# A fused attention and mixture-of-experts layer: head pairs as straight-line units, coarse scores in row tiles, routing moved among the attention units

## The chip, the core and the metric

The kernel runs on one core of one Trainium2 chip. Its time is device microseconds of that core, from launch to end, and lower is better. The core has five engines that run side by side and meet only at semaphores: TensorE (PE, matmuls into PSUM), VectorE (DVE), ScalarE (ACT), GpSimd (POOL) and SyncE (SP), which here issues all DMAs. PSUM has eight banks of 512 fp32 columns.

## The reference

Eight sequences of 512 tokens, width 128, pass one post-norm layer. Sixteen heads of width 64; eight experts of width 256, two of them chosen for each token.

```python
q, k, v = (einsum('bsd,hdk->bhsk', x, w) for w in (w_q, w_k, w_v))
weights = softmax(einsum('bhqk,bhmk->bhqm', q, k) / sqrt(64))
z = einsum('bhqm,bhmk->bhqk', weights, v)          # then heads side by side, times w_o
x1 = layernorm(x + (x + z @ w_o))
top_logits, top_idx = top_k(x1 @ gate_w, 2);  combine = one_hot(top_idx) * softmax(top_logits)
h = silu(einsum('bsd,edf->ebsf', x1, w1));  y = einsum('ebsf,efd->ebsd', h, w2)
out = layernorm(x1 + (x1 + einsum('ebsd,bse->bsd', y, combine)))
```

## The kernel before, in words

All data is fp32. Most matmul operands are split in a high part, rounded to the type fp32r, and a low part, the remainder; a `product` is three fp32r matmuls (high x high, high x low, low x high). `times_v` and `sum_probs` are plain fp32 matmuls, which the trace shows as two records each.

**Attention** goes over 64 head pairs n (8 sequences x 8 pairs). For a pair, q and k are projected as one 128-row tile (two heads of 64 rows) into the one bank `MISC`; ScalarE evicts the high part, VectorE the low one. SyncE then stacks high and low parts of each head by DMA into `q_stack` and `k_stack`, 128 rows for a head. *Coarse scores* (`coarse`, L519) are 8 matmuls a pair (2 heads x 4 tiles of 128 queries), from the stacks, into banks 4 and 5 in turn. VectorE reduces each to a row maximum (`maxima`, L1025), TensorE transposes the maxima (`shift_rows`, L537), VectorE copies them to a row (L1033), and a small DMA puts it into row 64 of the stack (`load_shift`, L284), so that the true scores (`scores`, L555 and L556) come out shifted. ScalarE takes exponentials of two banks at a time (`exps`, L858). GpSimd adds the four key tiles of each head (`add_probs`, L396). TensorE multiplies by v in four steps c that stand apart between other work (`times_v`, L567: two heads side by side, 64 output partitions each) and sums the probabilities over keys with a matrix of ones (`sum_probs`, L581), once a pair. ScalarE evicts the sums to `zT`, VectorE takes reciprocals in four pieces (L1040), and multiplies (`z_part`, L1045); ScalarE and VectorE split z (L871, L1050), TensorE projects out (`project_out`, L478 to L480) and VectorE adds into `acc` (L1061). All sequences are transposed at the start; `acc` holds all eight.

The order of work on each engine is written out by hand in `body(n, j)`. The first 8 and the last 2 pairs are straight-line, the rest a hardware loop over two pairs. Weights of a pair and x of a sequence are copied by DMA to fixed tiles (`load_wqk`, `load_wo`, `load_xT`), since a loop's addresses on TensorE are fixed.

**Experts** follow when attention has ended: steps k = 8b + e over sequences b and experts e (`chunk`). `hidden` (L478 to L480, 6 matmuls) runs three steps ahead, ScalarE applies silu into SBUF (L954), TensorE spreads the token weights c over partitions (`spread_c`, L725), VectorE gates (L1223), ScalarE and GpSimd split the result (`g_hi_part` L961, `g_lo_part` L426), and `second` (L735, L739) accumulates y over 8 experts. Among the steps stand, for later sequences: load of `acc`, transposes to tokens (L679), first norm (L1127, L1131, L1141, and GpSimd's power L422), transposes back, logits, routing (`route1` and `route2`, L1153 to L1185), transposed weights (`transpose_c`, L706); and for the former one the sum, second norm (L1232 to L1244) and store (L350).

## Time and profile before

| | |
|---|---|
| runs | median 1280.31 us of 3 (1279.3 to 1281.87) |
| profiled execution, span | 1280.0 us |
| busy: PE, DVE, ACT, POOL | 1196.7, 987.7, 602.0, 679.6 us |
| mean granted TensorE clock | 0.978 of full |
| moved by DMA | 153.47 MB |

The profile is of one execution. Busy time of an engine is the time in which an instruction of it ran; matmuls overlap, so a busy TensorE can still do more. "Idle before" is the time that the engine stood before an instruction, and the arrow names what ended it. A start-to-start distance in the timeline is what an instruction costs in a stream; its duration is longer, since it includes the way through the array. PE's granted clock has two levels, 1.2 and 2.4 GHz.

### The profile page before, as it was taken

Reading aid. Unit: us, or ns where it says so; the run is one execution under the profiler, and the core shown is the slowest. Engines: PE = TensorE matmul, PEld = TensorE weight load, DVE = VectorE, ACT = ScalarE, POOL = GpSimd, SP = SyncE. Lnnn points to the kernel's source line nnn. Section 1 sums busy time; section 2 is a strip of 40 time slices with the busy share of each in tenths; the row PEclk is TensorE's granted clock in tenths of the full one; section 3 lists DMA queues with packets and bytes.
Section 4 is the critical chain, followed back from the end, with each engine's and each line's share of the span. In section 5 each row is a group of like instructions: output and inputs, shape, how many; then the busy total and the mean of one; then the engine's idle time right before and its main releaser. Section 6 shows DMA issues by size and latency. Waiting matters only on the chain. (4 is left out here: it accounts for less than half of the span.)

```text
span 1280.0 us, 20247 instructions
## 1 busy us (share of the span) xinstructions
PE 1196.7 (93%) x4952; PEld 693.9 (54%) x4952; DVE 987.7 (77%) x1618; ACT 602.0 (47%) x744; POOL 679.6 (53%) x502
## 2 busy tenths in 40 slices
PE   5799999999999999999999999999998788888886
PEld 3454555555555555555555555555553566666664
DVE  4586888788888788888788888788887667777764
ACT  4444444444444444444444444444443555556553
POOL 0464644455544455544555544555546366666665
PEclk9898999999999999999999999999999889999999
DMA  9666666566665565665666665656660000000000
GB/s 213 162 161 153 157 155 157 144 156 147 157 156 140 144 155 146 158 159 153 150 150 153 159 148 140 150 149 152 160 161 21 21 9 17 17 17 16 8 9 17
DMA packets 91643, 153.47 MB, mean 120 GB/s; under 512 B 18016, under 2 KB 36960, under 8 KB 91616
## 3 DMA queue, kind: packets, MB, share of 16 engines
q1 hardware_dynamic: 91616, 153.14, 48.1%
q8 instruction: 13, 0.21, 0.1%
q14 instruction: 14, 0.11, 0.0%
HBM read 6.30 MB, written 2.10 MB: 7 GB/s over the span
## 5 line engine op out<-in xcount | busy, mean ns | idle before, releaser
L1025 DVE TENSOR_REDUCE neg_max<-psum 128x1 fp32r<-128x512 f32 x512 | 345.1, 680 | 114.1 <-PE psum L530 112.1
L1040 DVE RECIPROCAL zT<-zT 128x128 f32<-128x128 f32 x256 | 241.4, 944 | 4.2 <-ACT zT L865 2.2
L530 PE MATMUL psum<-k_stack,q_stack 128*128 128x512 f32 x512 | 224.6, 451 | 6.8 <-DVE neg_max L1025 1.4
L555 PE MATMUL psum<-q_stack,k_stack 128*128 128x512 f32 x512 | 210.5, 411 | 9.9 <-DMA q_stack<-q_stack 7.4
L858 ACT ACTIVATE probs_even<-psum 128x1024 f32<-128x1024 f32 x128 | 131.0, 1023 | 179.1 <-PE psum L556 179.1
L556 PE MATMUL psum<-q_stack,k_stack 65*128 65x512 f32 x512 | 205.2, 401 | 0.0
L396 POOL TENSOR_TENSOR probs_sum<-probs_even 128x512 f32<-128x512 f32 x64 | 82.5, 1289 | 227.4 <-PE psum L581 187.2
L396 POOL TENSOR_TENSOR probs_sum<-x_tok 128x512 f32<-128x512 f32 x64 | 82.2, 1284 | 226.9 <-PE psum L581 226.9
L530 PEld LDWEIGHTS psum<-k_stack,q_stack 128*128 128x128 f32 x512 | 97.1, 190 | 185.0 <-DVE neg_max L1025 87.9
L396 POOL TENSOR_TENSOR probs_sum<-probs_sum,probs_even 128x512 f32<-128x512 f32 x128 | 164.1, 1282 | 14.5 <-ACT probs_even L858 3.3
L396 POOL TENSOR_TENSOR probs_sum<-probs_sum,x_tok 128x512 f32<-128x512 f32 x128 | 164.3, 1283 | 11.3
L858 ACT ACTIVATE x_tok<-psum 128x1024 f32<-128x1024 f32 x128 | 130.9, 1023 | 41.7 <-PE psum L556 41.7
L567 PE MATMUL psum<-x_tok,v 128*64 128x512 f32 x512 | 139.7, 626 | 0.0
L567 PE MATMUL psum<-probs_even,v 128*64 128x512 f32 x512 | 137.9, 617 | 0.0
L1223 DVE TENSOR_TENSOR x_tok<-x_tok,psum 128x1024 f32<-128x1024 f32 x64 | 77.9, 1217 | 77.1 <-PE psum L725 48.1
L555 PEld LDWEIGHTS psum<-q_stack,k_stack 128*128 128x128 f32 x512 | 98.1, 192 | 45.8 <-issue 20.4
L865 ACT ACTIVATE zT<-psum 128x512 f32<-128x512 f32 x64 | 38.3, 598 | 171.0 <-PE psum L581 171.0
L556 PEld LDWEIGHTS psum<-q_stack,k_stack 65*128 65x128 f32 x512 | 98.0, 191 | 20.4
L426 POOL TENSOR_TENSOR k_stack<-x_tok,k_stack 128x1024 fp32r<-128x1024 f32 x32 | 76.9, 2404 | 54.6 <-ACT k_stack L961 54.6
L426 POOL TENSOR_TENSOR q_stack<-x_tok,q_stack 128x1024 fp32r<-128x1024 f32 x32 | 75.5, 2377 | 35.8 <-ACT q_stack L961 35.8
L847 ACT ACTIVATE v<-psum 128x1024 f32<-128x1024 f32 x32 | 32.9, 1027 | 128.5 <-PE psum L567 126.6
L954 ACT ACTIVATE x_tok<-psum 128x1024 f32<-128x1024 f32 x64 | 65.6, 1026 | 56.4 <-PE psum L480 55.4
(119 smaller groups left out, 1927.1 us busy)
## 6 DMA issues: line engine op xcount, KB each, us to landing
q_stack<-q_pair SPq DMA_DIRECT2D x128, 256.0 KB, 3.0
k_stack<-k_pair SPq DMA_DIRECT2D x128, 256.0 KB, 3.6
q_stack<-q_pair SPq DMA_DIRECT2D x128, 128.0 KB, 3.5
k_stack<-k_pair SPq DMA_DIRECT2D x128, 128.0 KB, 3.4
xT_cur<-xT SPq DMA_DIRECT2D x32, 512.0 KB, 3.0
wqk_cur<-w_tab SPq DMA_DIRECT2D x63, 256.0 KB, 3.3
wo_cur<-w_tab SPq DMA_DIRECT2D x64, 128.0 KB, 3.0
x_tok<-L_attn_x_dram SPq DMA_DIRECT2D x8, 256.0 KB, 5.4
```

Of the source, the lines that this page charges most:

```text
L396: nc.gpsimd.tensor_tensor(probs_sum[h][:], left, probs[j][:, h, c, :], ALU.add).then_inc(s["added"], 1)
L426: nc.gpsimd.tensor_tensor(g_lo[e % GB], gated[e % 2], bits(g_hi[e % GB]), ALU.subtract).then_inc(s["g_lo_done"], 1)
L530: nc.tensor.matmul(psum[:, COARSE + t % 2, :], q_stack[j][:, h, 0, t * P:(t + 1) * P], k_stack[j][:, h, 0, :], start=True, stop=True).then ...
L555: nc.tensor.matmul(psum[:, t, :], k_stack[j][:, h, 0, keys], q_stack[j][:, h, 0, :], start=True, stop=False)
L556: mm = nc.tensor.matmul(psum[:, t, :], k_stack[j][0:EXT, h, 1, keys], q_stack[j][0:EXT, h, 1, :], start=False, stop=True)
L567: mm = nc.tensor.matmul(psum[h * DK:(h + 1) * DK, Z, :], v[:, j, c, h, :], probs[j][:, h, c, :], start=(c == 0), stop=(c == TT - 1))
L858: nc.scalar.activation(probs[j][:, h, 2 * g:2 * g + 2, :], psum[:, 2 * g:2 * g + 2, :], ACT.Exp).then_inc(s["exp_done"], 1)
L865: nc.scalar.activation(zT[:], psum[:, MISC, :], ACT.Copy).then_inc(s["sums_out"], 1)
L954: nc.scalar.activation(silu[e % 2], psum[:, FC * (e % 2):FC * (e % 2 + 1), :], ACT.Silu).then_inc(s["silu_done"], 1)
L1025: nc.vector.tensor_reduce(neg_max[h][:, t:t + 1], psum[:, COARSE + t % 2, :], AX.X, ALU.max, negate=True).then_inc(s["max_done"], 1)
L1040: nc.vector.reciprocal(zT[:, cols], zT[:, cols]).then_inc(s["r_done"], 1)
L1223: nc.vector.tensor_tensor(gated[e % 2], silu[e % 2], psum[:, CB, :].unsqueeze(1).broadcast_to([P, FC, S]), ALU.mult).then_inc(s["gated"], 1)
```

## The change

The program is written anew. No hardware loops are left: every engine runs through units n = -2 .. 64 as straight-line code, then through 64 expert steps. The parts:

- `coarse` reads `q_pair` and `k_pair` (high parts only, 64 rows a head) instead of the stacks. The two heads' matmuls use rows 0 to 63 and 64 to 127 and write two banks; one `maxima` reduces both. One transpose and one row copy serve both heads.
- `times_v` of the former pair stands in one block, `sum_probs` once for two pairs, with 32 columns of ones, four tiles into one bank. ScalarE evicts 128 rows of sums, VectorE takes reciprocals (4 pieces for two pairs), and SyncE spreads them with 4 DMAs a pair (`spread_recip`). z is evicted by ScalarE (`z_part`), and GpSimd multiplies (`z_mul`) and makes the low part (`z_lo`).
- The copies of weights and x to fixed tiles are gone. x of later sequences is loaded and transposed among units; `acc` holds two sequences, and the first addition takes 2x in.
- First norm and routing of sequences 0 to 6 stand in attention units 8b + 11 to 8b + 15 (`norm_of`), those of the last one in the expert steps (`LAST_NORM`). The token weights go to DRAM and come back spread over 128 partitions (`spread_c`, by DMA). Logits are made with tokens on partitions.
- In the expert steps, silu is written in place in PSUM and the gate reads it there; y has two banks in turn.
- Experts' weights are loaded and split in four quarters in units 0 to 7.

The core of the diff, cut:

```diff
 # TensorE
-                nc.tensor.matmul(psum[:, COARSE + t % 2, :], q_stack[j][:, h, 0, t * P:(t + 1) * P], k_stack[j][:, h, 0, :],
-                                 start=True, stop=True).then_inc(s["coarse_done"], 1)
+            def coarse(m, t):
+                if t == 0:
+                    pe.wait_ge(s["qhi"], m + 1)
+                    pe.wait_ge(s["khi"], m + 1)
+                    n = m - 1
+                    if n > 0:
+                        pe.wait_ge(s["exp_done"], group(n - 1, 1, 1) + 1 if (n - 1) % 2 == 0 else group(n - 1, 0, 1) + 1)
...
+                for h in range(2):
+                    half = slice(h * DK, (h + 1) * DK)
+                    mm = nc.tensor.matmul(psum[:, coarse_pair(t) + h, :], q_pair[half, 0, t * P:(t + 1) * P], k_pair[half, 0, :],
+                                          start=True, stop=True)
+                mm.then_inc(s["coarse_done"], 1)
...
+            def times_v(n):
+                j = n % 2
+                pe.wait_ge(s["exp_done"], group(n, 1, 1) + 1)
+                pe.wait_ge(s["v_out"], n // 2 + 1)
+                wait(pe, s["acc_done"], n - 2)
+                pe.wait_ge(s["row_done"], min(n + 2, N))
+                for c in range(TT):
+                    for h in range(2):
+                        mm = nc.tensor.matmul(psum[h * DK:(h + 1) * DK, Z, :], v[:, j, c, h, :], probs[j][:, h, c, :],
+                                              start=(c == 0), stop=(c == TT - 1))
+                mm.then_inc(s["pv_done"], 1)
+            def sum_probs(k):
+                pe.wait_ge(s["added"], 6 * (2 * k + 2))
...
+                for i in range(4):
+                    mm = nc.tensor.matmul(psum[32 * i:32 * i + 32, M, :], ones[:], probs_sum[i // 2][:, i % 2, :], start=True, stop=True)
+            def project_out(m):
+                pe.wait_ge(s["zhi"], m + 1)
+                pe.wait_ge(s["zlo"], m + 1)
+                pe.wait_ge(s["row_done"], min(m + 5, N))
...
+            for n in UNITS:          # order of a unit (waits and bounds of n left out)
+                transpose_x(b), or to_tokens / transpose_x1 / logits / transpose_c of norm_of(n, step)
+                coarse(n + 1, 0); coarse(n + 1, 1)
+                times_v(n - 1)
+                if n % 2 == 0: sum_probs((n - 2) // 2)
+                coarse(n + 1, 2); coarse(n + 1, 3)
+                scores(n, 0, 0); project_q(n + 2); scores(n, 0, 1); project_k(n + 2); scores(n, 1, 0)
+                transpose_max(n + 1); project_out(n - 3); scores(n, 1, 1)
+                if n % 2 == 0: project_v(n)
 # ScalarE: order of a unit
+                z_part(n - 1); [even: sums_part((n - 2) // 2)]; zT_part(n - 3)
+                exps(n, 0, 0); q_part(n + 2); exps(n, 0, 1); k_part(n + 2)
+                exps(n, 1, 0); exps(n, 1, 1); [even: v_part(n)]
+            def zT_part(m):
+                act.wait_ge(s["zmul"], m + 1)
+                wait(act, s["wo_done"], m)
+                nc.scalar.activation(zT_hi[:], z_raw[:, m % 3, :], ACT.Copy).then_inc(s["zhi"], 1)
 # VectorE
-                    nc.vector.tensor_reduce(neg_max[h][:, t:t + 1], psum[:, COARSE + t % 2, :], AX.X, ALU.max,
-                                            negate=True).then_inc(s["max_done"], 1)
+                nc.vector.tensor_reduce(neg_max[:].rearrange("p (h t) -> p h t", h=2)[:, :, t], psum[:, bank:bank + 2, :], AX.X,
+                                        ALU.max, negate=True).then_inc(s["max_done"], 1)
+                maxima(n + 1, 0); maxima(n + 1, 1); [norm or routing part]; maxima(n + 1, 2); maxima(n + 1, 3)
+                q_part(n + 2); [even: reciprocal 0]; k_part(n + 2); row_part(n + 1); [even: reciprocal 1]
+                acc_part(n - 3); [even: reciprocals 2 and 3]
 # GpSimd: order of a unit
+                add_probs(n - 1, 1); [rstd_part(b)]; z_mul(n - 3); z_lo(n - 3); add_probs(n, 0)
+            def z_mul(m):
+                pool.wait_ge(recip_in[m % 2], 4 * DMA * (m // 2 + 1))
+                pool.wait_ge(s["z_out"], m + 1)
+                z = z_raw[:, m % 3, :]
+                nc.gpsimd.tensor_tensor(z, z, recip[:, m % 2, :], ALU.mult).then_inc(s["zmul"], 1)
 # SyncE
+            def spread_recip(m):
+                sp.wait_ge(s["recip_done"], TT * (m // 2 + 1))
+                wait(sp, s["zmul"], m - 1)
+                for h in range(2):
+                    i = 2 * (m % 2) + h
+                    for r in range(2):
+                        sp.dma_start(recip[h * DK + r * 32:h * DK + (r + 1) * 32, m % 2, :],
+                                     sums[32 * i:32 * i + 32, :]).then_inc(recip_in[m % 2], DMA)
+                [odd n: spread_recip(n - 3); spread_recip(n - 2)]; [expert quarter]
+                stack(0, n + 2, 0); shift(n + 1); stack(1, n + 2, 0); stack(0, n + 2, 1); stack(1, n + 2, 1)
 # expert steps
-                nc.scalar.activation(silu[e % 2], psum[:, FC * (e % 2):FC * (e % 2 + 1), :],
-                                     ACT.Silu).then_inc(s["silu_done"], 1)
+                nc.scalar.activation(h, h, ACT.Silu).then_inc(s["silu_done"], 1)      # h: the two PSUM banks
-                nc.tensor.matmul(psum[:, CB, :], select_e[:, e, :], cT[:, j, :], start=True,
-                                 stop=True).then_inc(s["cb_done"], 1)
+                sp.dma_start(c_b[:, e, :], c_dram[b, e:e + 1, :].broadcast_to([P, S])).then_inc(c_in[e], DMA)
+                nc.vector.tensor_tensor(gated[k % 2], psum[:, FC * (k % 2):FC * (k % 2 + 1), :],
+                                        c_b[:, e, :].unsqueeze(1).broadcast_to([P, FC, S]), ALU.mult).then_inc(s["gated_done"], 1)
```

The orders of a unit above are given as calls in a line; in the program each stands under its own condition on n. After the last unit the engines run the 64 expert steps: TensorE `hidden(k + 3)` and `second(k)`, ScalarE `silu_part(k + 2)` and `g_hi_part(k + 1)`, VectorE `gate_part(k + 2)`, GpSimd `g_lo_part(k)`, with the last two pairs' `z_mul`, `z_lo` and `project_out` among the first of them.

## Rows read from the trace of the kernel before

**Rows 1.** The page, parts 1 and 2: busy time and slices.
```profile
PE 1196.7 (93%) x4952; PEld 693.9 (54%) x4952; DVE 987.7 (77%) x1618; ACT 602.0 (47%) x744; POOL 679.6 (53%) x502
...
PEclk9898999999999999999999999999999889999999
```

**Rows 2.** Busy time in two stretches of the expert phase: PE, PEld, DVE, ACT, POOL, clock.
```profile
1100.00:1250.00 150.00, 131.68 (x563) 100.95 (x561) 106.71 (x202) 89.44 (x97) 94.23 (x52) 0.95 0.04 14
...
1097.00:1101.00 4.00, 3.81 (x12) 3.00 (x13) 3.13 (x11) 0.84 (x2) 1.29 (x3) 0.57 0.00 0
```

**Rows 3.** Timeline of TensorE, two head pairs in mid attention: start, duration, instruction.
```profile
501.87 0.28 PE L537 MATMUL psum<-ident,neg_max 128*4 128x128 f32 x1
...
502.69 0.40 PE L480 MATMUL psum<-xT,wqk_cur 128*128 x1
502.93 0.39 PE L530 MATMUL psum<-k_stack,q_stack 128*128 128x512 f32 x1
503.25 1.08 PE L567 MATMUL psum<-probs_even,v 128*64 128x512 f32 x4
...
526.68 0.28 PE L479 MATMUL psum<-w_tab,xT_cur 128*128 x1
526.80 0.28 PE L480 MATMUL psum<-w_tab,xT_cur 128*128 x1
...
531.33 0.28 PE L537 MATMUL psum<-ident,neg_max 128*4 128x128 f32 x1
```

**Rows 4.** Timeline of TensorE, last pairs: two steps of times_v together.
```profile
972.09 1.94 PE L567 MATMUL psum<-probs_even,v 128*64 128x512 f32 x8
...
973.86 1.03 PE L581 MATMUL psum<-probs_sum,ones 128*64 128x512 f32 x4
```

**Rows 5.** Groups by line and shape: busy us, mean ns, idle before and releasers.
```profile
L1025 DVE TENSOR_REDUCE neg_max<-psum 128x1 fp32r<-128x512 f32 x512 | 345.1, 680 | 114.1 <-PE psum L530 112.1
L1040 DVE RECIPROCAL zT<-zT 128x128 f32<-128x128 f32 x256 | 241.4, 944 | 4.2 <-ACT zT L865 2.2
...
L396 POOL TENSOR_TENSOR probs_sum<-probs_sum,x_tok 128x512 f32<-128x512 f32 x128 | 164.3, 1283 | 11.3
...
L858 ACT ACTIVATE probs_even<-psum 128x1024 f32<-128x1024 f32 x128 | 131.0, 1023 | 179.1 <-PE psum L556 179.1
...
L1223 DVE TENSOR_TENSOR x_tok<-x_tok,psum 128x1024 f32<-128x1024 f32 x64 | 77.9, 1217 | 77.1 <-PE psum L725 48.1 <-ACT x_tok L954 20.1 <-POOL q_stack L426 8.9
...
L426 POOL TENSOR_TENSOR q_stack<-x_tok,q_stack 128x1024 fp32r<-128x1024 f32 x32 | 75.5, 2377 | 35.8 <-ACT q_stack L961 35.8
...
L1012 DVE TENSOR_TENSOR k_pair<-psum,k_pair 128x512 fp32r<-128x512 f32 x64 | 40.5, 633 | 2.5 <-ACT k_pair L836 2.4
...
L831 ACT ACTIVATE q_pair<-psum 128x512 fp32r<-128x512 f32 x64 | 38.2, 597 | 4.7 <-PE psum L480 2.5 <-DMA q_stack<-q_pair 2.2
...
L1033 DVE CAST q_stack<-psum 4x128 fp32r<-4x128 f32 x128 | 36.2, 283 | 51.2 <-PE psum L537 49.1
...
L961 ACT ACTIVATE k_stack<-x_tok 128x1024 fp32r<-128x1024 f32 x32 | 33.7, 1054 | 1.0 <-DVE x_tok L1223 1.0
```

**Rows 6.** Expert phase: spread_c's first and last start, and TensorE's wait for routing.
```profile
L725 PE MATMUL psum<-xT_cur,k_pair x64: 389/396/776, 1001.5 to 1263.9; 128*128 128x512 f32 x64
...
1097.19 0.96 PE L706 MATMUL psum<-ident,probs_even 128*8 128x128 f32 x4 [3.98 <-DVE probs_even L1185]
```

**Rows 7.** DMA issues: line, count, KB each, median us from issue to landing.
```profile
q_stack<-q_pair SPq DMA_DIRECT2D x128, 256.0 KB, 3.0
...
probs_even<-acc SPq DMA_DIRECT2D x8, 256.0 KB, 2.3
...
acc<-L_attn_w_k_dram SPq DMA_DIRECT2D x1, 512.0 KB, 6.9
```

**Rows 8.** Timeline at the start: the first exponentials.
```profile
39.60 1.02 ACT L858 ACTIVATE probs_even<-psum 128x1024 f32<-128x1024 f32 x1 [6.20 <-PE psum L556]
```

**Rows 9.** Timeline at the end: the last expert matmuls.
```profile
1270.25 0.74 PE L739 MATMUL psum<-k_stack,w_tab 128*128 128x512 f32 x2 [0.68 <-POOL k_stack L426]
```

More of the change, by code:

```diff
@@ new lines, in has, with coarse_pair, score_banks, group @@
+        def has(m):
+            return 0 <= m < N
+        def coarse_pair(t):
+            return 2 + 2 * (t % 2)
+        def score_banks(n, h, g):
+            if h == 0:
+                return 0 if g == 0 else 2
+            if g == 0:
+                return 4
+            return 2 if n % 2 == 0 else 0
+        def group(n, h, g):
+            return 4 * n + 2 * h + g
+        def x_unit(b):
+            return -2 if b == 0 else 8 * (b - 1) + (0 if b == 1 else 2)
+        def x_of(n):
+            for b in range(B):
+                if x_unit(b) == n:
+                    return b
+            return None
@@ L208, in expert_quarter, with norm_of, quarter_at @@
+        def norm_of(n, step):
+            b, r = divmod(n - 11 - step, 8)
+            return b if r == 0 and 0 <= b < B - 1 else None
+        QUARTERS = 4
+        def quarter_at(n, first):
+            q, r = divmod(n - first, 2)
+            return q if r == 0 and 0 <= q < QUARTERS else None
         def expert_quarter(step):
@@ new lines, in _ @@
+            for n in UNITS:
+                if n % 2 and has(n - 3) and has(n - 2):
+                    spread_recip(n - 3)
+                    spread_recip(n - 2)
+                if (step := quarter_at(n, 0)) is not None:
+                    if step == 0:
+                        sp.wait_ge(s["xT_done"], 2)
+                    wait(sp, s["experts_lo"], step)
+                    half = slice(step % 2 * NE // 2, (step % 2 + 1) * NE // 2)
+                    sp.dma_start(w1_raw if step < 2 else w2_raw,
+                                 w1_dram[:, half] if step < 2 else w2_dram[:, half]).then_inc(s["experts_in"], DMA)
+                if has(n + 2):
+                    stack(0, n + 2, 0)
+                if has(n + 1):
+                    shift(n + 1)
+                if has(n + 2):
+                    stack(1, n + 2, 0)
+                    stack(0, n + 2, 1)
+                    stack(1, n + 2, 1)
+                if n % 8 == 0 and 2 <= n // 8 + 1 < B:
+                    load_x(n // 8 + 1)
+                if (b := norm_of(n, ROUTE_UNITS)) is not None:
+                    store_c(b)
@@ L482, in project_qk @@
-            def project_qk(which, m, j):
-                first = isinstance(m, int) and m < 2
-                w = [w_tab[:, m, which, part, :] if first else wqk_cur[j][:, which, part, :] for part in range(2)]
-                return product(psum[:, MISC, :], w, [xT[:, m // HP, part, :] for part in range(2)])
-            def project_q(m, i, j):
-                if isinstance(m, int) and m < 2:
-                    pe.wait_ge(s["w_split"], 1)
-                else:
-                    pe.wait_ge(wqk_cur_in[j], DMA * i)
-                wait(pe, s["k_hi_done"], m)
-                wait(pe, s["k_lo_done"], m)
-                project_qk(0, m, j).then_inc(s["q_done"], 1)
@@ L744, in sum_to_tokens @@
                 pe.wait_ge(s["sum_done"], b + 1)
[L746 removed]
+                pe.wait_ge(s["acc_done"], N)
+                wait(pe, s["norm2_done"], TT * b)
                 for t in range(TT):
[L748 to L755 removed]
```

1484 lines of the change are left out of this document (657 added, 827 removed).

## Prediction

> **What bounds the kernel now.** I read the page first: TensorE is busy 93% of 1280 us, VectorE 77%, the others about half, and the granted clock stays at the upper level but for the first and the last quarter [rows 1]. Busy time of pipelined matmuls overstates the work, so I went on to the timeline of TensorE in the middle of attention. Two head pairs take 29.46 us there, from 501.87 to 531.33, or 14.73 us a pair. A 128-row matmul of 512 columns starts 0.24 us after the one before it, one of 256 columns 0.12 us, and the first matmul of `times_v` (64 output partitions) comes 0.32 us after a full-width one, so a change of shape costs about 0.08 us [rows 3]. Counted that way a pair is 16 score matmuls (3.8), 8 coarse (1.9), 6 for q and k (1.4), 3 for the output (0.7), half of 12 short ones for v (0.7), 4 blocks of `times_v` at 1.0 (4.0), `sum_probs` (1.0) and two small transposes: 13.6 us of the 14.73. Attention is bound by TensorE, and by little else.
>
> The expert phase is not. A full-clock expert is 13 matmuls, 3.06 us, but the 63 steps from 1001.5 to 1263.9 take 4.16 us each [rows 6]. The loss comes once a sequence: TensorE sits for 3.98 us until VectorE has routed the next sequence (L706 waits for L1185) [rows 6], and runs at the lower level of the clock afterwards: 0.57 granted over the next four microseconds, 0.95 over 150 [rows 2]. VectorE is busy for 106.7 of those 150, so for 23.4 in a sequence of 8 x 4.16 = 33 us; 8 gatings of 1.22 are 9.8 of it, the other 13.6 are routing, norms and sums, in an order in which one holds up the other.
>
> **Part by part, attention on TensorE.** Coarse scores: 8 full-array matmuls become 4 pairs, 64 rows each, in two halves of the array and two banks. The trace shows no row-tiled matmul. Bounds: 0.24 us a pair if both stream together, 0.48 if one after the other. A 128-column weight load with 256 columns of stream fits in 0.12 us [rows 3], so two loads fit in 0.24; and `times_v`, tiled by columns, does overlap. I take 0.25: 1.0 us for 1.9. `times_v` in one block: two blocks that stand together at the end of attention take 1.77 us, from 972.09 to 973.86 [rows 4], so four take 3.5 for 4.0. `sum_probs` for two pairs uses four 32-column tiles: between 0.96 us (the step after 973.86, as now) and twice that; I take 0.96, every second pair, so 0.5 saved a pair. Output, q, k, v and scores stay. Work falls to about 11.9 us a pair. The norm and routing of seven sequences (16 transposes of 0.1 and 12 small products each) come in, and mostly fall into waits below.
>
> The Trainium skill (TensorEngine Tiling, Key Properties) says that a change of tiling mode drains TensorE. The 0.08 us [rows 3] agrees with that. Modes now change about 4.5 times a pair instead of 8, which this sum takes as a small gain; a dearer drain for the row mode stands under the rivals.
>
> **The other engines.** VectorE: 4 maxima over two banks for 8 over one; the nearest row for 1024 columns from PSUM is 1.22 us (L1223) against 0.68, so 4.9 for 5.4. Reciprocals halve: 4 x 0.94 for two pairs. z's product and low part go to GpSimd. Of the 13.6 us a sequence beside gatings, sums and second norm stay where they are (about 4), so some 9.5 come in, 1.2 a pair. About 10.5 us. GpSimd: 6 additions and 2 new ones at 1.28 to 1.33, 10.6 us. ScalarE about 7 [rows 5]. None is the bound by its sum, so order and latency decide, and I worked out when each step of a unit can start.
>
> **A unit's clock.** Set 0 where the first exponentials of a unit start. ScalarE, in its written order, does exponentials (next may start after 0.92), q high, exponentials, k high, which ends at 2.97. VectorE's k low ends at 3.64 and the row copy (`row_part`, 0.28) at 3.9 [rows 5]. Only then may `project_out` have bank 7: it starts at 3.95, about 0.6 us after TensorE got there. Then output 0.7, last scores 0.95, so 5.6. *Even unit:* `project_v` to 7.04, its eviction by ScalarE to 8.27, `times_v` from 8.3 to 11.8, two coarse pairs with their mode changes 0.6, first scores of the next unit 0.94 and 0.17 until they are visible: 13.5. *Odd unit:* the last exponentials end at 6.81, `times_v` to 10.35, `sum_probs` 11.3, coarse 11.9, scores 13.0. That would be 26.5 for two pairs, 13.25 a pair.
>
> But z now goes a long way. ScalarE's zT high stands ahead of the next unit's exponentials and waits for GpSimd's product, and that for reciprocals carried across partitions by DMA. In an even unit VectorE reaches the fourth reciprocal at 7.35. SyncE, at 0.6 us an issue, stacks q and k until 8.8, and then issues four transfers, the last at 10.6. Landing takes 2.3 us (L346's, idle queues) to 3.0 (stacks) [rows 7]; at 2.5 it is 13.1. Product to 14.4, zT high until 15.0, of which the next exponentials overlap a little: they start at 14.95 and not at 13.5. Two pairs are then 14.95 + 13.0 = 27.95, 14.0 each. Behind the waiting zT high stand all of ScalarE's work, and through q low and k low the maximum's transpose and the output. The detour gives back 0.75 us of the 1.5 saved. The second pair's reciprocals come 2.4 us later and are wanted a unit later, so that half is not late. VectorE's routing insertions (that 9.5 in three units of eight) end about when the maxima are wanted: half a microsecond at most, which I leave in the rounding.
>
> The same skill page (PSUM Bottleneck) says that tiling speeds TensorE but not the eviction of PSUM. The unit's clock agrees: the maxima give back 0.5 us of VectorE where TensorE gives 0.9, and the wait ahead of `project_out` is one for evictions.
>
> **Start.** First exponentials are at 39.6 us now [rows 8], behind a shift whose small transfer queues after 1 MB of x. Now only two sequences are loaded ahead. Loads and k's projection put coarse scores at 13 us; four maxima in turn 18.5; w's low parts and the gate table 22.3; q and k low 23.6; row and transfer 27.5; first scores 29. So 10 us less.
>
> **Experts.** Per expert `spread_c` goes: 12 matmuls, 2.82 us. Silu stays in PSUM, the gate reads there and takes c from SBUF, by a transfer 8 experts ahead (hidden). Loops: hidden, silu 1.03, gate 1.22, next hidden but one: 3.9 for two experts. Gate 1.22, g high 1.05, g low 2.38, next gate but one: 4.8 for two [rows 5]. Both lie below 2.82 each. What is left once a sequence is sums and second norm, about 4 us on VectorE. I take 2.93, no 4 us stall, no fall of the clock; 5 us more for the last sequence's routing, which stays in this phase. Entry: after the last unit's exponentials start, its sums are ready at 9.1, reciprocals at 14.5, and two rounds of transfer, product, high and low end at 22.6 and 25.8. TensorE waits nearly 10 us for `project_out`, is slow after it, and GpSimd's first g low comes behind: first expert done at +30. Then 63 x 2.93 = 185, 5 for routing, and 9 from the last expert matmul to the end, as now (1270.99 to 1280.0) [rows 9]: 229. Now that stretch is 1280.0 - (39.6 + 63 x 14.73 = 967.6) = 312.
>
> **Sum.** 29 + 63 x 14.0 (882) + 229 = **1140 us**, against the profiled execution's own span of 1280.0, which lies 0.3 us below the median, so the same forecast holds for the runs. Of the 140, 83 come from experts, 46 from attention, 11 from the start.
>
> **Rivals.**
> *The detour is not late.* If the reciprocals land by 11.6, attention is 63 x 13.25 = 835, total 1093. For it: SyncE now waits much for rows, so its queue has room; against: its order puts eight transfers behind four stacks. 0.15.
> *Row tiles don't pay.* If the halves stream in turn, the coarse pairs after `times_v` cost 0.5 more where nothing hides it, every second unit, 15 us; if each mode change costs 0.1 more, 28 us. 1155 to 1183. For: no row shows this mode. 0.17.
> *Experts stay bound by the chain over VectorE and GpSimd.* The 4.8 us loop has 0.8 us of slack for two experts, and each norm's insertion can take more than that; 3.3 us an expert adds 24: 1164. 0.15.
> *Slower.* The reciprocals' landing is the mechanism. A wait of 3 us or more stops TensorE as in the expert phase, where the clock fell after 3.98 us and the next four microseconds ran near half speed [rows 2, 6]. Each two units then cost 3 + 2 us: 1140 + 31.5 x 5 = 1298. It decides from a landing 3 us later than my 2.5; the weights' loads took 6.9 [rows 7], but those come from DRAM in a full queue. 0.06.
> *Little gained in attention.* More waits of the kind I found, unseen; a pair stays at 14.7: 1184 and, with the entry and experts worse as well, up to 1270. 0.05, of which 0.02 ends without a measurable change. A straight-line program fetching its instructions too slowly would look like this; the first eight pairs are straight-line already.
>
> **How the numbers follow.** My forecast has 0.42. Its own range, with landing 2.3 to 3.0 (32 x 0.5) and experts 2.82 to 3.1, is 1125 to 1160. The range of 8 in 10 takes in the first three rivals, and reaches from 1090 to 1205. 0.2% (2.6 us) is about what the runs can tell. Faster 0.92, same 0.02, slower 0.06.
>
> **What would show it.** Right: coarse matmuls of 64 rows in pairs starting under 0.03 us apart, 0.24 from pair to pair; eight groups of `times_v` in 3.5 us; unit lengths that alternate, the one after an even unit about 1.9 us longer, with ScalarE's zT high waiting for GpSimd and GpSimd for DMA; `project_out` waiting for the row copy; an expert in 2.8 to 3.0 us at the upper clock; a gap of about 10 us on TensorE at the entry. Wrong: coarse pairs 0.48 apart, equal units, GpSimd or VectorE named ahead of most of the experts' second products, or lower clock within attention.

## The result, and the profile after

The changed kernel takes 1307.97 us (median of 4 runs, 1303.69 to 1312.97) against 1281.09 for the kernel before in the same job (4 runs, 1279.3 to 1283.95): a ratio of 1.0207, 95% interval 1.0176 to 1.0238. It is 2.1% slower; I had put it at 1140 us and 11% faster, and slower at 0.06.

The page of the changed kernel, busy time and slices, then its chain of work:

```profile
PE 1097.5 (84%) x4864; PEld 674.1 (52%) x4864; DVE 753.5 (58%) x1038; ACT 593.9 (46%) x748; POOL 834.2 (64%) x624
...
PEclk9989899999989998999889999898889988889998
...
PE 41%; issue 21%; POOL 19%; ACT 9%; DVE 7%; SPq 1%; DMA 1%; ACTq 0%; POOLq 0%; DVEq 0%
```

TensorE and VectorE do less work than in [rows 1] (99 and 234 us less busy), as the change intends, and it is still slower. The clock row shows it first: digits of 8 stand all through attention, where [rows 1] has them only at the start and where the experts begin.

Where the time went, by first exponentials (timeline of ScalarE): the first pair's are at 30.61 (39.60 before, [rows 8]), the last pair's at 1060.55. So 63 units take 1029.9 us, 16.35 each, where [rows 3] shows 14.73 before, and the rest takes 243.5 us, where it was 312 by that same row. (The trace of before has the last pair's first exponentials at 971.07, so the forecast's 63 x 14.73 = 928 was 931.5 in truth, and its 312 was 309.) Experts gained what was forecast within 15 us, and attention lost 98 us, or 102 against 928, instead of gaining 46. Units 26 and 27 from the middle, then 29, 47 and 55 (a unit is even or odd by its number n), and all of attention, as busy time in stretches (PE, PEld, DVE, ACT, POOL, granted clock):

```profile
463.92:480.19 16.27, 13.96 (x70) 8.80 (x69) 13.01 (x25) 7.23 (x10) 10.75 (x10) 1.00 0.55 128
480.19:493.93 13.74, 12.30 (x61) 6.57 (x62) 7.65 (x10) 7.03 (x12) 10.75 (x9) 1.00 0.53 119
510.20:526.42 16.22, 14.39 (x55) 6.96 (x54) 5.96 (x11) 6.66 (x12) 10.60 (x9) 0.79 0.47 100
801.83:815.57 13.74, 10.55 (x52) 4.87 (x51) 6.15 (x8) 6.55 (x10) 10.72 (x9) 1.00 0.53 120
930.35:946.41 16.06, 13.36 (x52) 6.16 (x51) 6.16 (x8) 6.54 (x10) 10.69 (x9) 0.79 0.47 102
160.00:1060.00 900.00, 771.03 (x3509) 444.78 (x3506) 543.57 (x737) 389.92 (x523) 572.20 (x459) 0.93 0.50 114
```

Units alternate, as forecast: 16.27 for an even one, 13.74 for an odd one (14.95 and 13.0 forecast). But an odd unit at a granted clock of 0.79 lasts about 16, and 0.93 is the mean over attention. The prediction had named a lower clock within attention as a sign that it is wrong. The waits (what waits, for what: us in all, times, longest):

```profile
POOL z_raw L338 <- DMA recip<-sums: 132.2, 32, 7.9
ACT zT_hi L748 <- POOL z_raw L338: 104.4, 31, 10.6
...
DVE q_pair L851 <- ACT q_pair L705: 91.2, 56, 5.4
...
PE psum L123 <- DVE q_stack L871: 42.0, 28, 1.6
PE psum L460 <- DVE q_pair L851: 40.1, 26, 4.0
```

Read from the top it is one chain: GpSimd's product waits for the spread reciprocals, zT high for the product, ScalarE's next work (exponentials, q high) for zT high, VectorE's q low for that, and TensorE for q low (bank Z, the maxima's transpose) and for the row copy. The timeline of unit 26, even, from 463.92 (SyncE's stretch is 8 transfers in 5.21 us):

```profile
473.50 0.61 SPq L207 DMA_DIRECT2D k_stack<-k_pair  x1
...
474.20 5.21 SPq L224 DMA_DIRECT2D recip<-sums  x8
...
478.35 1.27 POOL L338 TENSOR_TENSOR z_raw<-z_raw,recip 128x512 f32<-128x512 f32 x1 [0.92 <-DMA recip<-sums]
...
479.65 0.63 ACT L748 ACTIVATE zT_hi<-z_raw 128x512 fp32r<-128x512 f32 x1 [2.64 <-POOL z_raw L338]
...
480.19 1.00 ACT L729 ACTIVATE probs<-psum 128x1024 f32<-128x1024 f32 x1
```

The last k stack is issued at +9.6 and the spread starts at +10.3, where I had 8.8: an issue costs SyncE about 0.65 us (5.21 for 8) and the row's transfers 1.33 for two. The product starts at +14.4 (13.1 forecast). And what a stall then does, in unit 29, behind an even unit whose zT high started at 509.66:

```profile
512.56 0.27 PE L460 MATMUL psum<-ident,neg_max 128*8 128x128 f32 x1 [0.30 <-DVE q_pair L851]
...
514.34 0.77 PE L123 MATMUL psum<-zT_hi,w_tab 128*128 128x512 f32 x1 [1.51 <-DVE q_stack L871]
...
514.90 0.63 PE L124 MATMUL psum<-zT_lo,w_tab 128*128 128x512 f32 x1
...
515.33 0.63 PE L125 MATMUL psum<-zT_hi,w_tab 128*128 128x512 f32 x1
...
515.76 0.63 PE L483 MATMUL psum<-q_stack,k_stack 128*128 128x512 f32 x1
```

From 512.26 to 514.34 TensorE had one small transpose to do; then 128x512 matmuls start 0.43 us apart instead of 0.23 and last 0.63 instead of 0.40: the lower of its two levels, 1.2 GHz. Measured in the same way, such a stretch is 1.4 us in the even unit 26 and 1.6 us in unit 27, and the clock stayed. But its length does not decide. In units 47 and 55 it is the same, 2.94 and 2.95 us:

```profile
804.20 0.27 PE L460 MATMUL psum<-ident,neg_max 128*8 128x128 f32 x1 [1.17 <-DVE q_pair L851]
805.97 0.47 PE L123 MATMUL psum<-zT_hi,w_tab 128*128 128x512 f32 x1 [1.51 <-DVE q_stack L871]
...
932.71 0.27 PE L460 MATMUL psum<-ident,neg_max 128*8 128x128 f32 x1 [1.18 <-DVE q_pair L851]
934.48 0.77 PE L123 MATMUL psum<-zT_hi,w_tab 128*128 128x512 f32 x1 [1.51 <-DVE q_stack L871]
```

In both the output starts 4.13 to 4.14 us after the unit's first exponentials, and up to there they run alike. In unit 47 the clock stayed and the unit lasts 13.74 us; in unit 55 it fell and the unit lasts 16.06. So it is over the 27 odd units from 9 to 61. In all of them the output starts at +4.13 to +4.18. The 8 that kept the upper level last 13.74 to 13.76 us, with stretches of 1.6 to 2.95 us; the 19 in which the clock fell last 14.8 to 16.5, with stretches of 2.1 to 4.6 us. Against 13.74 these 19 lose 38.6 us. In an odd unit the wait itself costs nothing, the fall behind it costs 2.0 us on the mean.

What was forecast right: TensorE's row tiles. A coarse block of two pairs (L452) starts at 507.00 and the scores behind it at 507.67 (below, beside the run that undoes it). `times_v` takes 3.58 us (3.5 forecast), `sum_probs` 1.0, the maxima 1.220 us each.

### The profile page after: what moved, and what is told of

It is laid out like the page before. It is cut to its first block, busy times and chain, and to the rows that moved or that the text cites. A ratio compares the mean times of both kernels' runs of the same rounds, so it can differ in the third digit from the quotient of the medians.

```text
span 1304.1 us, 16364 instructions
## 1 busy us (share of the span) xinstructions
PE 1097.5 (84%) x4864; PEld 674.1 (52%) x4864; DVE 753.5 (58%) x1038; ACT 593.9 (46%) x748; POOL 834.2 (64%) x624
## 4 chain that ended last, share of the span: by engine, by line
PE 41%; issue 21%; POOL 19%; ACT 9%; DVE 7%; SPq 1%; DMA 1%; ACTq 0%; POOLq 0%; DVEq 0%
PE psum L509 9%; PE psum L483 7%; PE psum L484 7%; ACT probs L729 6%; POOL probs_sum L332 6%; PE psum L123 4%; POOL k_stack L380 4%; POOL q_stack L380 4%; PE psum L452 3%; PE psum L125 3%; PE psum L124 3%; POOL z_raw L338 3%; PE psum L520 2%; DVE neg_max L865 2%; ACT k_pair L711 1%
## 5 line engine op out<-in xcount | busy, mean ns | idle before, releaser
L865 DVE TENSOR_REDUCE neg_max<-psum 128x2 fp32r<-128x1024 f32 x256 | 302.4, 1220 | 200.5 <-PE psum L452 200.5
L332 POOL TENSOR_TENSOR probs_sum<-probs_sum,probs 128x512 f32<-128x512 f32 x256 | 325.7, 1272 | 107.8 <-ACT probs L729 83.4
L729 ACT ACTIVATE probs<-psum 128x1024 f32<-128x1024 f32 x256 | 262.3, 1025 | 212.9 <-PE psum L484 206.6
L509 PE MATMUL psum<-probs,v 128*64 128x512 f32 x1024 | 247.3, 626 | 11.4 <-issue 6.0
L332 POOL TENSOR_TENSOR probs_sum<-probs 128x512 f32<-128x512 f32 x128 | 163.8, 1280 | 52.4 <-ACT probs L729 52.4
L338 POOL TENSOR_TENSOR z_raw<-z_raw,recip 128x512 f32<-128x512 f32 x64 | 81.5, 1274 | 132.2 <-DMA recip<-sums 132.2
L343 POOL TENSOR_TENSOR zT_lo<-z_raw,zT_hi 128x512 fp32r<-128x512 f32 x64 | 82.1, 1282 | 98.1 <-ACT zT_hi L748 98.1
L876 DVE RECIPROCAL sums<-sums 128x128 f32<-128x128 f32 x128 | 116.5, 932 | 9.0 <-ACT sums L743 8.0
L123 PE MATMUL psum<-xT,w_tab 128*128 128x512 f32 x256 | 105.9, 414 | 9.0 <-DVE probs L1016 4.4
L452 PE MATMUL psum<-k_pair,q_pair 64*128 64x512 f32 x512 | 105.4, 491 | 3.8 <-DVE neg_max L865 3.1
L125 PE MATMUL psum<-xT,w_tab 128*128 128x512 f32 x256 | 103.9, 406 | 0.0
L124 PE MATMUL psum<-xT,w_tab 128*128 128x512 f32 x256 | 103.9, 406 | 0.0
```

The source lines that it names most:

```text
L123: nc.tensor.matmul(dst, lh, rh, start=True, stop=False)
L124: nc.tensor.matmul(dst, lh, rl, start=False, stop=False)
L125: return nc.tensor.matmul(dst, ll, rh, start=False, stop=True)
L332: nc.gpsimd.tensor_tensor(probs_sum[j][:, h, :], left, probs[j][:, h, c, :], ALU.add).then_inc(s["added"], 1)
L338: nc.gpsimd.tensor_tensor(z, z, recip[:, m % 2, :], ALU.mult).then_inc(s["zmul"], 1)
L452: mm = nc.tensor.matmul(psum[:, coarse_pair(t) + h, :], q_pair[half, 0, t * P:(t + 1) * P], k_pair[half, 0, :], start=True, stop=True)
```

## Experiments

All ratios are to the kernel before, with 95% intervals; the changed kernel stands at 1.0207. Attention is T0 to T63, the first exponentials of the first and the last pair.

**No detour.** `spread_recip` issues nothing; `recip` is set once to a constant, and the next eviction of sums waits for the reciprocals and not for their transfers. The output is not normalised. With the wait, SyncE's 256 issues go too.

```diff
-                for h in range(2):
+                for h in range(0):
...
-                pool.wait_ge(recip_in[m % 2], 4 * DMA * (m // 2 + 1))
...
+            nc.gpsimd.memset(recip[:], 0.002).then_inc(s["recip_set"], 1)
```

> The changed kernel without the spreading of reciprocals: no DMA of it is issued, and GpSimd multiplies z by a tile of constants, so that its product waits for z alone (the output is then not normalised). The reciprocals are still taken. Theory A: everything that the detour costs goes, the unit's clock is the one worked out without it (13.7 and about 14.1 us), the clock stays up, and the kernel takes 1150 to 1190 us. If e1 is near this, order was all of it; if e2 is well below e1, the late product also holds up the output and GpSimd. Theory B: 1260 us or more.

Measured 1205.49 us, ratio 0.9401 (0.9386 to 0.9417), 15 us above the range. Attention is 940.6 us instead of 1029.9, and what follows it 233.2 instead of 243.5: the detour costs 89 us there and 10 at the entry to the experts. The stretch of attention in this run:

```profile
160.00:950.00 790.00, 701.18 (x3420) 410.44 (x3416) 533.58 (x724) 386.63 (x509) 555.35 (x446) 1.00 0.49 110
```

The clock is whole here; it is lower only in seven of the first eight units and in unit 62. Quiet units (without norm and routing) are 14.4 and 14.0, so 28.4 a pair against 16.27 + 13.74 = 30.0: 1.6 us x 32 = 52 us are plain waiting, which is near the 47 that I had (1.5 x 31.5). The other 37 of attention appear only together with the lower clock. Unit by unit: the 32 even units are 63.4 us longer in the changed kernel, at the upper level in all but the last; 19 odd ones that ran low there and at the upper level here are 32.6 longer; the other 12 odd ones are 6.6 shorter. The 32.6 is from the 14.0 of this run, the 38.6 above from the changed kernel's own 13.74.

**zT high behind the exponentials.** `zT_part(n - 3)` moves from ahead of `exps(n, 0, 0)` to behind `q_part(n + 2)` on ScalarE.

> The changed kernel with ScalarE's order in a unit altered: zT_part(n - 3) stands behind exps(n, 0, 0) and q_part(n + 2) and not ahead of them. Theory A, the z detour: what makes a unit after an even one long is that zT high, waiting for GpSimd's product and so for the reciprocals' DMA, holds back the first exponentials; the clock falls because of that. It expects an even-to-odd distance of first exponentials of 14.1 to 14.5 us where it is 16.3 now, 29 us or less for two units, and 1190 to 1225 us in all with fewer stretches at the lower clock. Theory B, bank 7: the wait of project_out for the row copy is what stalls TensorE and lets the clock fall. It expects that stall and the clock to stay, and 1270 us or more.

Measured 1253.92, 0.9802 (0.9767 to 0.9836), between the ranges of both theories; attention is 977.1 us, at a clock of 0.98. One line of order is worth 54 us and by itself turns the change from a loss into a gain of 2%. From unit 8 on most units are at the upper level and 14.6 to 15.7 us long. The clock is low in the first eight, whose odd ones last 18 to 25 us, and which together are 5 us longer than in the changed kernel.

**Spread earlier.** In an even unit SyncE spreads one pair's reciprocals ahead of the last k stack and the other's behind it, instead of both in the next odd unit's turn.

```diff
-                if n % 2 and has(n - 3) and has(n - 2):
-                    spread_recip(n - 3)
-                    spread_recip(n - 2)
...
                     stack(0, n + 2, 1)
+                if n % 2 == 0 and n < N and has(n - 2):
+                    spread_recip(n - 2)
+                if has(n + 2):
                     stack(1, n + 2, 1)
+                if n % 2 == 0 and n < N and has(n - 2):
+                    spread_recip(n - 1)
```

> The changed kernel with SyncE's order altered alone: in an even unit the first pair's reciprocals are spread ahead of the last k stack, and the second pair's right behind it, and not both at the head of the next unit. Theory A, the z detour through a late place in SyncE's queue: the product of an odd unit starts about 2 us earlier, zT high no longer holds back the exponentials, units after an even one fall from 16.3 to about 14.5 us, and the whole takes 1210 to 1240 us. Rival: the k stack, now 2.7 us later, holds back k's high part through its buffer, and nothing is gained (1280 us or more).

Measured 1241.76, 0.9682 (0.9644 to 0.9721), 2 us above the range. Its waits:

```profile
POOL z_raw L340 <- DMA recip<-sums: 81.5, 27, 7.4
...
ACT zT_hi L750 <- POOL z_raw L340: 54.1, 31, 10.0
```

Both are about 50 us shorter than in the changed kernel, and the time is 66 us shorter. The late thing was the place in SyncE's queue, not the landing, which is 2.0 us in the changed kernel's page (2.5 forecast) and 2.2 us here.

**Output before the maxima's transpose**, so that `project_out` doesn't wait for the row copy of bank 7; `acc_part` goes ahead of `row_part`. Bank 7 holds q's projection, the maxima and the output in turn, so the edit also brings waits: `project_out` (first lines of the diff) now waits for q low, and the transpose for the addition into `acc`.

```diff
-                pe.wait_ge(s["row_done"], min(m + 5, N))
+                pe.wait_ge(s["row_done"], min(m + 4, N))
+                pe.wait_ge(s["qlo"], min(m + 6, N))
...
-                if has(n + 1):
-                    transpose_max(n + 1)
                 if has(n - 3):
                     project_out(n - 3)
                 if has(n):
                     scores(n, 1, 1)
+                if has(n + 1):
+                    transpose_max(n + 1)
```

> The changed kernel with project_out(n - 3) and the last scores ahead of the maxima's transpose, and the addition into acc ahead of the row copy: project_out no longer waits for the row. Theory B: 1.2 us less in every unit and no fall of the clock, 1190 to 1230 us. Theory A: units after an even one stay at 16 us, since zT high still waits; the others gain up to 1 us, and the total stays above 1260 us.

Measured 1317.56, 1.0291 (1.0269 to 1.0312): slower still. Its waits:

```profile
POOL z_raw L338 <- DMA recip<-sums: 186.4, 32, 8.2
ACT zT_hi L750 <- POOL z_raw L338: 177.9, 32, 10.8
DVE q_pair L853 <- ACT q_pair L707: 158.8, 56, 6.7
...
PE psum L123 <- DVE q_pair L853: 102.0, 30, 5.5
```

The theory that the row copy holds the unit falls, as far as this run can tell: the 42 us of waiting for it are gone, and 102 us of waiting for q low, a wait that the edit brings in, stand in their place. Both waits are at the end of the chain that starts at the reciprocals, and the earlier links are longer than before. The clock over attention is 0.90.

**Both heads on the same rows.** Row tiling undone: both heads' coarse matmuls read rows 0 to 63.

```diff
+                    half = slice(0, DK)
                     mm = nc.tensor.matmul(psum[:, coarse_pair(t) + h, :], q_pair[half, 0, t * P:(t + 1) * P], k_pair[half, 0, :],
```

> The changed kernel with both heads' coarse matmuls on the data and rows of head 0, so that the two of a pair cannot run side by side in the array (the maxima of head 1 are then those of head 0). Theory C, row tiles bring nothing: no change of time. Theory A with working row tiles: each pair of coarse matmuls takes 0.24 us more, 0.96 us a unit, of which the half after times_v counts where nothing hides it: 15 to 60 us more.

Measured 1338.2, 1.0421 (1.0399 to 1.0443), some 30 us above the changed kernel, in the range. (The profile is of its slowest execution, 1352.69.) A coarse block and the matmul behind it, here:

```profile
500.29 1.19 PE L453 MATMUL psum<-k_pair,q_pair 64*128 64x512 f32 x4
501.41 0.50 PE L484 MATMUL psum<-q_stack,k_stack 128*128 128x512 f32 x1
```

and in the changed kernel:

```profile
507.00 0.73 PE L452 MATMUL psum<-k_pair,q_pair 64*128 64x512 f32 x4
...
507.67 0.50 PE L483 MATMUL psum<-q_stack,k_stack 128*128 128x512 f32 x1
```

The block takes 0.67 us with row tiles and 1.12 without. Two halves do stream at once. The even units from 8 on are as long as before in sum (465 us in both), since the wait for z covers the difference; all of the loss is in odd units. At the upper level they last 13.74 us before and 14.2 to 14.5 here, and the 19 at the lower one 14.8 to 16.5 before and 15.6 to 19.4 here.

**A filled wait.** The matmuls of `scores(n, 1, 0)`, which stand ahead of the waits at the transpose and the output, are issued twice: 256 instructions more, 0.9 us a unit.

```diff
-                for i in range(2):
+                for i in list(range(2)) * (2 if (h, g) == (1, 0) else 1):
```

> The changed kernel with more work for TensorE: the four matmuls of scores(n, 1, 0) are issued twice, into the same banks, so that the stalls ahead of the maxima's transpose and of project_out have 0.94 us of work in them. Theory, the clock: in about half of the odd units the clock falls after these stalls (granted 0.79 in such a unit, 1.00 in others) and costs 1.5 to 2 us; the filling keeps it up in some of them and the kernel gets 5 to 45 us faster though it does more. Rival: the fall has nothing to do with the stall, and the work costs up to 0.94 us a unit, 10 to 60 us more.

Measured 1301.56, 1.0151 (1.0125 to 1.0177). With 64 x 0.94 = 60 us more work on TensorE the kernel is no slower than the changed one, 6 us less by the medians (the intervals just touch). All of attention:

```profile
160.00:1060.00 900.00, 804.90 (x3721) 477.74 (x3722) 544.80 (x741) 392.52 (x524) 574.58 (x460) 0.96 0.50 115
```

The clock is 0.96 where the changed kernel has 0.93. This profile is of an execution of 1310.06 us, the slowest of the four, and the changed kernel's of one of 1305.93; but the mean clock of whole executions is 0.950 to 0.957 in all four here and 0.928 to 0.934 there. From unit 9 on the clock falls in 13 odd units instead of 19, and they lose 21.1 us instead of 38.6. Odd units at the upper level last 13.76 us with the added work and 13.74 without it, so there it is free. Even ones pay 0.4 us for it, 17.63 for 17.22. That a fuller TensorE keeps its clock more often is what this run shows; that the kernel gains by it in all is within the noise.

**Logits' exponentials first.** `exp_logits(b)` ahead of `z_part` and `sums_part` on ScalarE. VectorE's `route_weights` waits for it, and behind `route_weights` stand two maxima. The maxima's transpose now also waits for z's eviction, which frees its bank.

> The changed kernel with the exponentials of the router's logits at the head of ScalarE's unit, ahead of z and sums; TensorE's transpose of the maxima waits for z's eviction, which the old order implied. Theory: VectorE waits 4.1 us for them in each of seven units (28.9 us in the profile), and these units are 18.0 us long and not 16.3. I expect 10 to 20 us less in all. Rival: VectorE has that slack and only the z detour counts, no change.

Measured 1289.31, 1.0062 (1.0038 to 1.0087): 19 us. The profiles have 15 us of it in the seven units with these exponentials: six of 18.0 to 18.6 us are 1.6 to 1.8 shorter, and the last, of 17.2, is 4.9 shorter and no longer at the lower clock.

**The orders together.** Spread earlier and logits' exponentials first:

> The earlier spread of the reciprocals and the earlier exponentials of the logits together, without the move of the experts' low parts. If the two effects are separate and add up, 1241.8 (earlier spread) less 19 gives 1223. If the earlier spread had already taken the cover of the logits' stall (both act at TensorE's clock), 1235 or more. The distance from here to the version that also moves the low parts of the experts' weights (1204.4) is what those low parts cost on GpSimd: 19 us by the first theory, and it should lie in the units 0 to 8 alone, which last 19 us in the changed kernel where odd units take 14 later.

Measured 1222.95, 0.955 (0.9523 to 0.9578): the two effects add up (1223 expected). And with `expert_lo` moved from GpSimd to VectorE, behind the second maximum:

> Both orders of the two runs before together (reciprocals spread earlier, the logits' exponentials first), and the experts' weights' low parts (four of 2.4 us on GpSimd in the first eight units) moved to VectorE, which takes 1.2 us and stands ahead of the third maximum. If the three costs are separate, 25 to 35 us below the run with earlier spreading alone: 1180 to 1210 us. If they hide one another, within 10 us of it.

Measured 1204.36, 0.9405 (0.9383 to 0.9428), 6% faster than the kernel before. By its median it is the best of the versions that compute the whole layer. Of the 18.6 us since the last run, 16.9 are in units 0 to 8; TensorE's wait for the sums of probabilities falls from 11.6 us to 2.6. Its page:

```profile
PE 1042.1 (87%) x4864; PEld 647.5 (54%) x4864; DVE 772.2 (64%) x1042; ACT 598.9 (50%) x748; POOL 830.1 (69%) x620
...
PEclk9989999999998999999999999999999979999998
```

From this version, three more. Without the detour:

> The version with all three changes of order, and z times a constant in place of the reciprocals carried by DMA (the reciprocals are still computed; the output is not normalised by the sums). It shows what is left of the detour's cost in that version. If the detour is hidden by then, but for the units of 15.8 and 16.2 us: 1204 less at most 20, so 1185. If it still acts through the clock or through SyncE's queue: 1165 or less. The floor of my unit's clock without detour, 13.25 us a pair, would give 1103 to 1120; I expect quiet pairs of units at 28.0 to 28.4, as in the first run without the detour, so that 14.1 us a unit is the work and waits that I had put at 13.25.

Measured 1169.19, 0.9118 (0.9091 to 0.9145). Between the two expectations: 24 us of attention (928.4 to 904.1) and 6 behind it are left of the detour, by the profiles; by the medians it is 35 in all. This is the floor of the unit's order, and its quiet pair of units still takes 28.38 us:

```profile
487.49:501.89 14.40, 12.79 (x64) 8.11 (x63) 10.57 (x13) 7.22 (x9) 10.21 (x9) 1.00 0.55 128
501.89:515.87 13.98, 12.80 (x64) 6.98 (x63) 7.66 (x10) 7.28 (x10) 10.13 (x9) 1.00 0.52 114
```

With the output before the transpose again (the edit above):

> The version with all three changes of order, and project_out and the last scores ahead of the transpose of the maxima, the sum into acc ahead of the row copy. In the changed kernel this order cost 9.6 us, which I put down to z arriving late: project_out then waited for z where the transpose would have gone first. Theory: with z earlier, project_out's operands are there, so the wait for bank 7 (the row copy, about 0.6 us a unit) goes, and the time falls by 10 to 30 us, to 1175 to 1195. Rival: the row is wanted by SyncE and the next scores as early as now, so a later transpose moves the wait to the first scores: 1204 or up to 1220.

Measured 1205.78, 0.9399 (0.9366 to 0.9433): no change, the rival's answer. Odd units fall from 13.7 to 15.2 us to 12.6 to 14.9, even ones rise from 14.6 to 15.8 to 15.7 to 17.3, and zT high waits 125 us for its product instead of 51. The clock falls in 17 of the 27 odd units from 9 to 61, where it fell in 2, and is 0.96 over attention instead of 0.99. The 10 that keep it last 12.65 us; this order gives to odd units what it takes from even ones, and a clock that falls more often. With zT high behind the exponentials:

> The version with all three changes of order, and ScalarE's high part of z behind the first exponentials and q's high part. Theory: in it ScalarE still waits 51 us for GpSimd's product ahead of the exponentials, in the repeating units of 15.8 and 16.2 us; with the high part behind the exponentials these fall to about 14.4 to 15, so 16 x 1.2 = 19 us less: 1185. Rival: the wait for z only moves on to project_out, which stands on TensorE ahead of the last scores: 1200 or above.

Measured 1209.08, 0.9441 (0.9418 to 0.9464): no gain, the rival again. Counted by first exponentials, the units of norm and routing (18 to 21, for one) last 14.7, 15.4, 15.4 and 14.6 us for 15.3, 14.4, 15.1 and 15.1, and the quiet pair becomes 29.3 us for 28.5; the repeating units of 15.8 and 16.2 that this expectation and the one without the detour speak of are in neither trace, only single ones. The clock is 1.00 over attention, so it is not what takes the gain away. The same edit was worth 54 us while the spread was late: which order is right depends on what is late.

## Why the prediction was wrong, by its own steps

The forecast 29 + 882 + 229 = 1140 stands against the profiled 30.6 + 1029.9 + 243.5 = 1304.0. Of these 164 us, 148 are attention, and the runs split them (the table's first line is the version with all orders, without detour, whose output is not normalised):

| step | forecast | measured | from |
|---|---|---|---|
| 63 units without detour, orders mended | 835 | 904.1 | orders together, without detour |
| routing and quarters in the wrong place (14.7 from unit 8 on, 21.7 before) | 0 | 36.5 | 940.6 - 904.1 |
| the detour | 47 | 89.3 | 1029.9 - 940.6 |

So more than one term of the sum was wrong. The largest error in size is in the first line, 69 us: the floor of a unit, 59, and 15 for insertions, less 5 in short units. Then come the detour, 42, what stood in the wrong place, 37, and the experts, 14.5. All are below. With all but the detour as measured and the detour as I priced it, the sum is 1262, which is outside my range too, but 18 us faster than before and not slower.

**The step that failed**, and that turned the gain into a loss, is "The detour gives back 0.75 us of the 1.5 saved": a late z was priced as a wait in ScalarE, passed on once. Its waiting was nearly of the size that I gave it, 52 us for 47. What I left out is that the same lateness opens gaps on TensorE, at the transpose and at the output, and that the clock falls there. That was my "slower" rival, with the right place and consequence, and I gave it 0.06 since I let it begin only with a stall of 3 us, taken from the one fall in the trace of before [rows 2, 6]. One example of a fall at 3.98 us bounds nothing from below, and I used it as a threshold. Here it fell after gaps of 0.30 and 1.51 us around one small transpose, and in other units it did not fall after 1.17 and 1.51. The rival's own trigger, a late landing, didn't happen; transfers landed in 2.0 us.

The split into 52 of waiting and 37 of clock is worked out, from quiet units and the rest. The trace of the changed kernel bears it out: units 47 and 55, alike in every wait, differ by 2.3 us, and the 19 odd units in which the clock fell lose 38.6 us against those in which it stayed. What decides whether it falls in a unit is left open: the length of the stretch before does not, and nothing else was tried but adding work. The Trainium skill (TensorE: Matmul & The Clock Gate, A second HAM failure mode: psum-queue depth-cycling) says, of a bf16 matmul kernel that goes through PSUM's banks in turn, that frequent short idles between groups of matmuls make the clock oscillate. The trace agrees, with 0.93 over 900 us and waits of 0.3 to 4.0 us, though 8 of 27 odd units kept the upper level.

**The floor of a unit**, 13.25 forecast and 14.19 measured in a quiet pair: short steps came out a little long, and all stand in one line. In the even unit from 487.49, the output starts at +4.37 (3.95), since k high ends at 3.13 (2.97), k low takes 0.69 (0.63), and the row copy is visible 0.2 us after its end; the last scores end at 6.07 (5.6), `times_v` starts at 8.83 (8.3) and ends at 12.42 (11.8), a coarse block with its changes of shape is 0.67 (0.6), and from there to the exponentials 1.3 (1.1). Sum 0.9 in an even unit, 1.0 in an odd one, 59 us in 63 units; with 15 for the insertions (below) and 5 back in shorter first and last units, that is the 69 of the table. The conclusion that the row copy costs what it is waited for would not follow: with that wait exchanged for others, nothing was gained, twice. The floor rests on one quiet pair, read step by step; no run shortens a step. (The work of a pair, put at 11.9 us in the prediction, adds up to 11.7 by its own terms; nothing in the sum rests on it.)

**Insertions.** "Half a microsecond at most, which I leave in the rounding" was wrong. In the floor version even units with norm and routing last 15.4 and 15.1 instead of 14.4, and with the odd ones beside them that is 2.2 us for each of seven sequences. In the changed kernel the logits' exponentials add 19 us, and the experts' low parts on GpSimd 18.6 (1222.95 - 1204.36), since they hold up the sums of probabilities in units 0 to 8 (16.9 of the 18.6). I had costed the quarters' loads and not their GpSimd work.

**Experts.** 8 experts take 23.5 us in the later sequences, 2.93 each, as forecast:

```profile
1204.00:1237.00 33.00, 30.99 (x140) 25.14 (x139) 20.34 (x36) 21.70 (x22) 28.62 (x16) 1.00 0.34 98
...
1105.00:1138.00 33.00, 28.27 (x117) 21.93 (x117) 19.61 (x42) 17.99 (x20) 20.67 (x12) 0.90 0.19 61
```

The second row is where the last sequence's norm and routing stand. The first 18 steps take 71.8 us and not 52.7; I had allowed 5 for that. TensorE waits for the sum of the first sequence there, and the clock falls again:

```profile
1124.34 0.66 PE L658 MATMUL psum<-ident,probs 128*128 128x128 f32 x4 [2.80 <-DVE probs L1024]
...
1125.46 0.63 PE L125 MATMUL psum<-xT,w_tab 128*128 128x512 f32 x1
```

From the last pair's first exponentials to the end of the first expert it took 33.4 us (30), of which the detour is some 10; TensorE's longest gap there is 5.9 us and not 10. The 63 experts behind took 200.8 us (185 and 5), and from the last expert matmul to the end it was 9.4 (9). The start was 30.6 (29).

**Right:** the start, row tiles at twice the rate, `times_v` in one block, the gate's and silu's new places, the alternation of units and the chain that makes it (GpSimd waiting for the transfers, zT high for GpSimd), and the gain of the expert phase but for 14.5 us. What the change is worth in all, 77 us, is seen only once the three orders are mended. That the waiting came out at 52 us where I had 47 is partly luck: it comes from an even unit of 16.3 against 14.4 where I had 14.95 against 13.5, and an odd unit that is 0.3 shorter than without detour. The rival of a straight-line program that fetches its instructions too slowly was not tested by itself; the floor version is straight-line too, and has its clock at 1.00 and 14.19 us a unit.

## What to carry to other kernels

When a value leaves for another engine by DMA and comes back, price the place in the issuing queue and everything that waits in written order behind its consumer, and then ask at which point TensorE runs dry: here the lateness was paid twice, once as a wait (52 us) and once as a clock at the lower level (37 us). Take away the first link of a chain of waits, not the last one that the profile names on the busiest engine. A stall seen once gives a length at which the clock fell, never one below which it is safe. To price the clock, compare units of one trace that are alike in their waits and not in their clock.

## What the hardware showed unexpectedly

- 60 us of extra matmuls in attention left the kernel no slower (1301.56 for 1307.97 us), with the granted clock at 0.96 for 0.93.
- The clock fell after 2.1 us in which TensorE had one small transpose (512.26 to 514.34), and fell in one unit and not in another after 2.95 us of the same. With the same waits, these two units last 16.06 and 13.74 us.
- The same matmuls in two row halves of the array: 0.67 us for four with the changes of shape, 1.12 us when all use one half.
- SyncE issued 8 small transfers in 5.2 us, 0.65 each; 64 KB between partitions landed in 2.0 us, less than the 2.3 of [rows 7].
